# A new head for a grouped-query attention block with layer norms: host-laid-out weights, high parts stacked first, float32r masks, unrolled batches

## The reference, cut to what matters

```python
def layernorm(x, eps=1e-5): return (x - mean(x)) / sqrt(var(x) + eps)
def attn(x, wq, wk_down, wv_down, wk_up, wv_up, wo):      # x: (4, 1024, 256)
    q = x @ wq                                            # 8 heads of 128, 4 for each of 2 kv heads
    k = (x @ wk_down per kv head, 32 wide) @ wk_up        # to 128
    v = (x @ wv_down per kv head, 32 wide) @ wv_up
    p = softmax(where(causal, q @ k.T / sqrt(128), min))
    return (p @ v) @ wo
x = x + attn(layernorm(x), ...)
x = x + ffn(layernorm(x))
# the ffn is a routed attention whose softmax runs over the batch, followed by a layer norm with ln_g, ln_b
```

## Time and profile before

| | |
|---|---|
| runs, us | 547.71, 540.63, 546.01; median 546.01 |
| the profiled execution | 546.95 us, of which the span of the trace is 545.2 us |
| mean granted TensorE clock | 0.886 |
| PE busy | 479.8 us (88%) |
| DVE, ACT, POOL busy | 336.9, 227.2, 231.1 us |
| DMA | 27.29 MB, 50 GB/s over the span |

### The profile page before, as it was taken

How to read it: one execution, slowest core, us unless ns; L and a number is a source line. 1 busy time by engine, 2 the same in 40 slices (tenths; PEclk the granted TensorE clock), 3 DMA queues, 4 the chain that set the end, 5 groups by cost and what they waited for, 6 DMA issues and landing times.

```text
span 545.2 us, 8184 instructions
## 1 busy us (share of the span) xinstructions
PE 479.8 (88%) x2722; PEld 257.9 (47%) x2722; DVE 336.9 (62%) x513; ACT 227.2 (42%) x428; POOL 231.1 (42%) x166
## 2 busy tenths in 40 slices
PE   4869697989999979999999799999997998799671
PEld 3537354544465535544655455444654464334240
DVE  5443567475455897885456978875469689701423
ACT  2300221535445434554454445554554345456300
POOL 2110104024543564526433953375328445743922
PEclk9675757779999979999999899999999899989866
DMA  9790720003501441009005410073054100100011
GB/s 290 217 139 22 94 24 1 2 1 65 82 2 26 54 71 40 2 28 151 9 2 73 73 40 1 0 143 41 1 73 68 46 2 1 39 2 0 1 38 39
DMA packets 20910, 27.29 MB, mean 50 GB/s; under 512 B 2897, under 2 KB 12945, under 8 KB 20881
## 3 DMA queue, kind: packets, MB, share of 16 engines
q1 hardware_dynamic: 19584, 25.60, 25.7%
q10 hardware_dynamic: 1296, 1.31, 0.8%
HBM read 6.72 MB, written 4.19 MB: 20 GB/s over the span
## 4 chain that ended last, share of the span: by engine, by line
PE 59%; issue 15%; DVE 13%; DMA 4%; ACT 3%; POOL 3%; SPq 1%; ACTq 1%; POOLq 0%; DVEq 0%
PE st_ps L447 12%; PE mx_ps L465 12%; PE u_ps L487 10%; PE sh_ps L498 6%; DVE mx_part L814 5%; PE sh_ps L564 5%; PE mx_ps L469 3%; PE sh_ps L532 3%; DMA qs<-q_lo 3%; DVE y L894 2%; PE sh_ps L525 2%; DVE y L903 2%; PE sh_ps L537 2%; ACT pr L680 1%; DMA pr<-in_wq 1%
## 5 line engine op out<-in xcount | busy, mean ns | idle before, releaser
L814 DVE TENSOR_REDUCE mx_part<-mx_ps 128x2 f32<-128x1024 f32 (+3 forms) x160 | 176.5, 1114 | 95.2 <-PE mx_ps L469 66.1
L680 ACT ACTIVATE pr<-st_ps 128x512 f32<-128x512 f32 (+1 forms) x304 | 168.5, 574 | 154.5 <-PE st_ps L447 146.8
L1064 POOL TENSOR_TENSOR pr<-pr 128x768 f32<-128x768 f32 (+3 forms) x72 | 154.4, 2149 | 73.5 <-ACT pr L680 71.7
L465 PE MATMUL mx_ps<-ks,qs 96*128 96x512 f32 (+3 forms) x384 | 133.3, 426 | 23.3 <-DVE mx_part L814 16.9
L447 PE MATMUL st_ps<-qs,ks 98*128 98x512 f32 (+1 forms) x304 | 143.0, 485 | 5.1 <-ACT pr L680 3.5
L1051 POOL TENSOR_SCALAR_AFFINE_SELECT pr<-pr 128x512 f32<-128x512 f32 x64 | 43.3, 676 | 163.4 <-ACT pr L680 163.2
L465 PEld LDWEIGHTS mx_ps<-ks,qs 96*128 96x128 f32 x384 | 84.1, 224 | 40.3 <-DVE mx_part L814 28.1
L447 PEld LDWEIGHTS st_ps<-qs,ks 98*128 98x128 f32 x304 | 60.0, 203 | 85.0 <-ACT pr L680 42.4
L487 PE MATMUL u_ps<-pr,v 128*32 128x512 f32 (+3 forms) x768 | 88.5, 535 | 6.2 <-POOL pr L1051 6.2
L469 PE MATMUL mx_ps<-maskb,identb 128*128 128x128 bf16 x256 | 63.7, 255 | 0.0
L1042 POOL TENSOR_TENSOR rstd<-var,minus_half 128x4 f32<-128x4 f32 (+1 forms) x13 | 15.5, 1189 | 70.8 <-DVE var L845 55.2
(11 more groups left out here) (82 smaller groups left out, 361.7 us busy)
## 6 DMA issues: line engine op xcount, KB each, us to landing
qs<-q_hi SPq DMA_DIRECT2D x32, 256.0 KB, 5.6
qs<-q_lo SPq DMA_DIRECT2D x16, 256.0 KB, 6.9
out_y<-y SPq DMA_DIRECT2D x8, 512.0 KB, 3.0
x<-in_x SPq DMA_DIRECT2D x3, 1024.0 KB, 11.4
ks<-k_hi SPq DMA_DIRECT2D x32, 64.0 KB, 3.3
x<-in_x SPq DMA_DIRECT2D x2, 512.0 KB, 7.3
pr<-in_wq ACTq DMA_DIRECT2D x1, 1024.0 KB, 6.5
pr<-in_wo SPq DMA_DIRECT2D x1, 1024.0 KB, 8.8
```

The lines of the kernel that those rows point to most:

```text
L465: last = nc.tensor.matmul(bank[:, i * pitch:i * pitch + width], qs[g][0:KS, t // CT, h0 + i, t % CT * P:(t % CT + 1) * P], ks[g][0:KS, k0: ...
L680: nc.scalar.activation(pr[:, slot, h0:h0 + nh, off:CH], st_ps[n % 2][:, 0:nh * width].rearrange("p (h q) -> p h q", h=nh), ACT.Exp, scale= ...
L814: nc.vector.tensor_reduce(mx_part[:, t // CT, own, h0:h0 + nh, t % CT], mx_ps[n % 2][:, 0:nh * pitch].rearrange("p (h k) -> p h k", h=nh)[ ...
L1064: last = nc.gpsimd.tensor_tensor(even, even, pr[:, 6 + (e // 2) % 2, h0:h1, off:CH], ALU.add)
```

## The change

The host hands over `wq` by head and transposed, and the two up-projections transposed; the kernel loads them so, and the head's transposes of `wq` and `up` go. ACT starts the weight loads, SP those of x of batch 0, now in four pieces of two tiles. The head's order is new: x first, `wq` folded in two halves (`wq0`, `wq1`), `qb0` ahead of the first mx units, and four more mx units (6 to 9, `MX_EARLY`) in the head instead of the first window's first three tiles. x of batches 1 to 3 is loaded later, between and behind the stacks, and so are ln_g and ln_b. DMAs of high parts start when ACT has written the high part (`stack_hi`), those of low parts when DVE has written the low part (`stack_lo`), in the head and in every batch. The statistics of batch 1 stay at the head's end, those of batches 2 and 3 move to tile 1 of the second window of batches 0 and 1. The tiny `var` operations move from DVE to POOL, ahead of each power. The mask matmul takes float32r operands and covers all heads of a unit that lie in one PSUM bank (4, 2, 1, 1 heads at 128, 256, 384, 512 columns), 22 of them a window instead of 32. The loops are written out.

```diff
-MX_AT_FIRST = [5, 5, 4, 3, 2, 3, 3, 3, 2, 2, 1, 1]
+MX_AT_FIRST = [4, 4, 2, 3, 2, 3, 3, 3, 2, 2, 1, 1]
+MX_EARLY = 4
...
-USES_START = ["wqT0", "wqT1", "wqT2", "wqT3", "upT", "wq", "xT0", "xT1", "k0", "qa0", "xT2", "xT3",
-              "k1", "qa1", "wo", "v", "m0", "qb0", "qb1"]
-SETUP = USES_START.index("xT0")
+USES_START = ["xT0", "xT1", "k0", "wq0", "qa0", "xT2", "xT3", "k1", "qa1", "wq1", "qb0", "v", "m0", "qb1", "wo"]
...
+        minus_half = sb("minus_half", [P, TT])
         lng = sb("lng", [P, D])
         lnb = sb("lnb", [P, D])
         wqk = sb("wqk", [P, ND, NH * DL])
...
-            for c in range(NC):
-                sp.dma_start(x[:, 0, c * CT:(c + 1) * CT, :],
...
+            for i in range(2 * NC):
+                sp.dma_start(x[:, 0, 2 * i:2 * i + 2, :],
+                             x_d[0].rearrange("(i t p) d -> i p t d", t=2, p=P)[i]).then_inc(x0_in[i], 16)
             sp.dma_start(wo_in, wo_d.rearrange("(h p) n -> p h n", p=P)).then_inc(wo_loaded, 16)
-            for b in range(1, B):
...
+                for kind, g, c in pieces:
+                    s = slice(c * CH, (c + 1) * CH)
+                    if kind == "k":
+                        sp.wait_ge(hi_ready, nb * 6 + (1, 3)[c])
+                        for piece in (0, 2):
+                            sp.dma_start(ks[g][piece * DL:(piece + 1) * DL, s].bitcast(F),
+                                         k_hi[g * DL:(g + 1) * DL, s].bitcast(F)).then_inc(kstack_in[g][c], 16)
+                    else:
+                        sp.wait_ge(hi_ready, nb * 6 + ((2, 4), (5, 6))[g][c])
+                        for piece in (0, 1):
+                            sp.dma_start(qs[g][piece * DL:(piece + 1) * DL, c, :, :].bitcast(F), q_hi[:, s].bitcast(F)
+                                         ).then_inc(qstack_in[g][c], 16)
...
+            stack_hi(0, ("k", 0, 0), ("q", 0, 0))
+            wait_start(sp, "k0")
+            stack_lo(("k", 0, 0))
+            wait_start(sp, "qa0")
+            stack_lo(("q", 0, 0))
+            stack_hi(0, ("k", 0, 1), ("q", 0, 1))
+            wait_start(sp, "k1")
+            stack_lo(("k", 0, 1))
+            wait_start(sp, "qa1")
+            stack_lo(("q", 0, 1))
+            load_x(1)
+            stack_hi(0, ("k", 1, 0), ("q", 1, 0))
+            wait_start(sp, "qb0")
+            stack_lo(("k", 1, 0), ("q", 1, 0))
+            stack_hi(0, ("k", 1, 1), ("q", 1, 1))
+            wait_start(sp, "qb1")
+            stack_lo(("k", 1, 1), ("q", 1, 1))
             sp.dma_start(lng[:, :], lng_d[None, :].to_broadcast([P, D])).then_inc(ln_in, 16)
             sp.dma_start(lnb[:, :], lnb_d[None, :].to_broadcast([P, D])).then_inc(ln_in, 16)
...
-                s = slice(c * CH, (c + 1) * CH)
-                for piece, src in enumerate((q_hi, q_hi, q_lo)):
-                    sp.dma_start(qs[g][piece * DL:(piece + 1) * DL, c, :, :].bitcast(F), src[:, s].bitcast(F)
...
-            wait_start(sp, "k0")
-            stack_k(0, 0)
-            wait_start(sp, "qa0")
-            stack_q(0, 0)
-            wait_start(sp, "k1")
-            stack_k(0, 1)
-            wait_start(sp, "qa1")
-            stack_q(0, 1)
-            stack_k(1, 0)
-            stack_k(1, 1)
-            wait_start(sp, "qb0")
-            stack_q(1, 0)
-            wait_start(sp, "qb1")
-            stack_q(1, 1)
+            for b in range(2, B):
+                load_x(b)
...
-                stack_k(0, 1)
-                wait_apart(sp, (sh_read, use_no(b, 0, kind, "qa1") + 1))
-                stack_q(0, 1)
-                wait_apart(sp, (st_full, w * NST + (NST + ST_END[3])),
-                           (sh_read, use_no(b, 1, kind, "qb0") + 1))
...
+                sp.wait_ge(st_full, w * NST + ST_END[7])
+                stack_hi(b + 1, ("k", 0, 0), ("q", 0, 0))
+                sp.wait_ge(sh_read, use_no(b, 0, kind, "k0") + 1)
+                stack_lo(("k", 0, 0))
+                sp.wait_ge(sh_read, use_no(b, 0, kind, "qa0") + 1)
+                stack_lo(("q", 0, 0))
+                sp.wait_ge(st_full, w * NST + NST)
+                stack_hi(b + 1, ("k", 0, 1), ("q", 0, 1))
...
+                sp.wait_ge(st_full, w * NST + (NST + ST_END[7]))
+                stack_hi(b + 1, ("q", 1, 0), ("k", 1, 0))
+                sp.wait_ge(sh_read, use_no(b, 1, kind, "qb0") + 1)
...
-                    last = nc.tensor.matmul(bank[:, i * pitch:i * pitch + width],
-                                            qs[g][0:KS, t // CT, h0 + i, t % CT * P:(t % CT + 1) * P],
-                                            ks[g][0:KS, k0:k0 + width], start=True, stop=not own)
+                together = max(1, CH // pitch) if own else 1
+                for i0 in range(0, nh, together):
+                    heads = range(i0, i0 + together)
+                    for i in heads:
+                        last = nc.tensor.matmul(bank[:, i * pitch:i * pitch + width],
+                                                qs[g][0:KS, t // CT, h0 + i, t % CT * P:(t % CT + 1) * P],
+                                                ks[g][0:KS, k0:k0 + width], start=i == i0, stop=not own)
                     if own:
-                        last = nc.tensor.matmul(bank[:, i * pitch + width - P:i * pitch + width],
-                                                identb[:, :], maskb[:, :], start=False, stop=True)
+                        diagonals = bank[:, i0 * pitch:(i0 + together) * pitch].rearrange(
+                            "p (h k) -> p h k", h=together)[:, :, width - P:width]
+                        last = nc.tensor.matmul(diagonals, ident_r[:, :], mask_r[:, 0:together, :], start=False, stop=True)
                 last.then_inc(mx_full, 1)
...
             pe.sem_inc(pv_done, PV_AHEAD)
+            def fold(name):
+                starting(name)
+                if name == "wq0":
+                    pe.wait_ge(wq_in, 16)
+                g = int(name[-1])
+                for d in range(ND):
+                    for h in range(HG):
+                        last = nc.tensor.matmul(start_bank(name)[:, (d * HG + h) * DL:(d * HG + h + 1) * DL],
+                                                wqT[:, g * HG + h, d * P:(d + 1) * P], upT[:, 0, :], start=True, stop=True)
...
-            last.then_inc(sh_full, 1)
-            for name in USES_START[SETUP:]:
-                if name == "wo":
+            for name in USES_START:
+                if name == "v":
                     for i in range(MX_C0):
                         mx(0, 0, 0, i)
+                if name == "wo":
+                    for i in range(MX_C0, MX_C0 + MX_EARLY):
+                        mx(0, 0, 0, i)
+                if name[:2] == "wq":
+                    fold(name)
+                elif name == "wo":
...
-            wait_start(pe, USES_START[-2])
-            wait_start(pe, USES_START[-1])
+                else:
+                    fill(name, None, 0, 0, 0)
...
                         st(wn, 1 - g, n)
             batch(0, FIRST)
...
-            act.dma_start(wq_in_sb, wq_d.rearrange("(c p) n -> p c n", p=P)).then_inc(wq_in, 16)
+            act.dma_start(wkd[:, :, :], wkd_d.rearrange("(c p) n -> p c n", p=P)).then_inc(weights_in, 16)
+            act.dma_start(wvd[:, :, :], wvd_d.rearrange("(c p) n -> p c n", p=P)).then_inc(weights_in, 16)
+            act.dma_start(upT[:, :, :], up_d).then_inc(weights_in, 16)
...
                     last = nc.vector.bn_stats(st1[:, b, t, :], x[:, b, t, :])
-                last.then_inc(ln_step, 1)
-                dve.wait_ge(ln_step, 2 * count - 1)
+                last.then_inc(stats_step, 1)
+                dve.wait_ge(stats_step, count)
                 for t in tiles:
                     last = nc.vector.bn_aggr(mv1[:, b, t, :], st1[:, b, t, :])
-                last.then_inc(ln_step, 1)
-                dve.wait_ge(ln_step, 2 * count)
-                nc.vector.tensor_scalar(var1[:, b, tiles[0]:tiles[-1] + 1], mv1[:, b, tiles[0]:tiles[-1] + 1, 1], EPS, None,
-                                        ALU.add).then_inc(var_ready, 1)
+                last.then_inc(stats_ready, 1)
...
                     last = nc.vector.bn_aggr(mv2[:, t, :], st2[:, t, :])
-                last.then_inc(ln_step, 1)
-                dve.wait_ge(ln_step, steps + 2)
-                nc.vector.tensor_scalar(var2[:, :], mv2[:, :, 1], 1.0 + EPS, EPS * EPS, ALU.mult, ALU.add
-                                        ).then_inc(var_ready, 1)
+                last.then_inc(var_ready, 1)
             def norm2_apply(b, c, powers, steps, t, last_half):
...
                         dve.wait_ge(out_done, y_count(b, c) * 16)
...
+            nc.vector.memset(ones[:, :], 1.0).then_inc(consts_ready, 1)
             for c in range(NC):
-                dve.wait_ge(x0_in[c], 16)
-                norm1_stats(0, range(c * CT, (c + 1) * CT), c + 1)
-            for c in range(NC):
-                dve.wait_ge(rstd_ready, c + 1)
+                for i in range(2):
```

(34 more changed lines are left out.)

185 lines of the change are left out of this document (87 added, 98 removed).

## The result

The changed kernel takes **526.55 us** (median of 4 runs, 523.31 to 528.19) and the kernel before 546.12 (4 runs beside it, 540.63 to 547.71). The ratio is 0.9655, 95% interval [0.9596, 0.9713]: faster. The forecast was 531, with a range of 517 to 541.

What follows compares the result with a forecast made beforehand. PE, busy 88% of the span, was taken to set the pace, with its losses in the first 120 us. 546.95 - 4.9 (head) - 4.5 (units) - 2.0 (masks) - 4.6 (windows) + 0.3 (tail) = 531.3, so 531 us, range 517 to 541.

Steps and rivals of the forecast that it cites:

- The head: Start to resumption of DVE's maxima: earlier q_hi and SP's DMA queue move the resumption from 65.0 to 60.1, -4.9 us.
- my 60.1: Head: ln_b, last in SP's queue, lands at 24.0 + 2.65 + 33.4 = 60.1 us, when DVE resumes its maxima.
- v at half clock: Head: sign of being wrong; in the rival where the head gains nothing, resumption at 65, sum 536, chance 0.20.
- Four units less: First window of batch 0: mx units 6 to 9 leave its first three tiles, which ran at 0.50 clock, -4.5 us.
- Masks: Row-sum windows: grouped mask matmuls save 0.24 us a window, -2.0 us with the stretches at half clock.
- The "slower" rival: Masked matmuls: the float32r mask's weight load is never hidden, 176 x 0.137 = 24 us at full clock, total 559; chance 0.05.
- Windows: First windows of batches 1 to 3: var on POOL and earlier stacks save 1.3, 1.3 and 2 us, -4.6 us.
- The moved statistics: Second windows: 3.4 us of DVE and under 2 of POOL each cost 0; 5.4 each if nothing covered them.
- the gap of PE: Second windows: sign of being wrong, if the moved statistics open a gap of PE there.
- Loops: Windows: writing the loops out gains 0, since windows written out and inside the loop were 0.05 us apart.
- The clock, as a rival: First window: PE kept from falling to 1.2 GHz, up to 19 us gained, two thirds give 518; chance 0.15.

Runs made afterwards that it cites:

- experiment 6: Changed kernel with identity and mask in bf16 instead of float32r, masks still grouped: 526.22 us (521.91 to 529.37).
- experiment 4: Changed kernel without the four early mx units in the head, which go back into the first window: 529.04 us, one run of 536.78 left out.
- experiment 2: Changed kernel with the masks as before, bf16 and one matmul for each head: 526.09 us (523.27 to 528.45).
- experiment 3: Changed kernel with the variance's small operation back on VectorE: 529.31 us (528.77 to 533.97), one run of 538.54 left out.
- experiment 8: Changed kernel with each stack's three pieces copied together behind the low part: 524.25 and 516.72 us, runs of 526.63 and 531.70 left out.
- experiment 5: Changed kernel with x of batch 0 loaded in two pieces of 512 KB, not four of 256 KB: 518.41 us (516.41 to 521.49).
- experiment 7: Changed kernel without the moved statistics; batches 2 and 3 are normalised with those of batch 1: 517.64 us (512.35 to 518.36).
- experiment 10: Changed kernel with x in two pieces and idle matmuls at three kinds of places where TensorE waits: 517.48 us (515.26 to 517.77).
- experiment 9: Changed kernel, x in four pieces, with two idle memsets on VectorE delaying the first statistics by 0.9 us: 528.01 us (523.71 to 530.10).
- experiment 11: Changed kernel with x in two pieces and the layer norm's loads right behind wo_in: 520.77 us (517.96 to 524.97), one run of 527.34 left out.
- experiment 1: Changed kernel with the layer norm's gain and bias loads moved right behind wo_in: 526.18, 527.93, 528.08 us and one run of 515.28.

## Why the prediction was right, and where it was not

**The head (-4.9; it was -9.5).** The mechanism stands: the queue of copies decides, DVE waits for ln_b. From q's first copy to the resumption I had 36.1 us, and it was 34.7 (20.75 to 55.48). The step that failed is the start: I took the landing of x at 7.6 from the earlier trace rows and changed only the number of tiles behind it. x landed at 4.0, because the change also moves the small weights to ACT's queue ahead of wq (2.6 us, weights and wq together) and cuts the piece (0.9). Of these 3.6 us only 2.0 reached k, which began at 11.32 for my 13.3: the power covers four tiles and waits for the statistics of both pieces (rstd is used at 7.72, 3.7 us behind the first statistic, for my 2.4). And from k to q's high part it was 8.8 us for my 10.0, since PE had reached full clock by then (the four matmuls of q take 1.96 us, where they took 3.18 in the kernel before). That is 2.0 + 1.2 + 1.4 = 4.6 us under my 60.1, and the last two terms are partly luck: in the same head in experiment 6 k to q's high part took 9.5 us, and with v at half clock the maxima resumed at 58.70, nearer to my figure. I had named v at half clock as a sign of being wrong and priced it at a resumption of 65; it came in nine of the experiments' profiles, and since the whole head is earlier it costs about 3 us there and not the whole gain.

**Four units less (-4.5; the first window gave -7.4).** Taken alone they gave 2.5 us in the medians and 6.7 in the profiles (experiment 4), and my figure lies between. Over the window the clock is 0.80 in place of 0.76, which has its share in the 7.4; how large it is, no run shows.

**Masks (-2.0).** 0.24 a window by my sum, 0.3 by experiments 2 and 6 at full clock. In the total it can't be seen. The "slower" rival (weight load never hidden, 0.05) is refuted: the load is twice as long, and the window shows nothing of it.

**Windows (-4.6, from var and the stack together).** The variance is worth 1.3 us a window at full clock and 2.8 us in the medians, which is not clear of their spread (experiment 3); the stacks' order is worth nothing in the windows (experiment 8). So the 1.3 a window was of the right size and belongs to var alone. It shows where the clock is the same: the first window of batch 1 went from 55.74 us at 1.00 to 54.36 at 0.99, and the forecast said 54.5. The other two did not shrink. That of batch 2 takes 56.78 us at 0.97, where the kernel before had 55.73 at 1.00, and that of batch 3 takes 53.65 at 0.84, where it had 49.80 at 0.98. The step that failed is that I left the clock behind the first window as it was.

**The moved statistics (0).** Wrong: about 2 us, and the gap of PE that I had named as a sign of being wrong is there (4.52 us of idling, 3.57 without them). I argued from DVE's 37.43 busy us of 56.93; but in the second windows PE waits for DVE's maxima at places, and a share of busy time doesn't tell where.

**Loops (0).** The unrolled kernel was not run apart from the rest; the windows of both kernels agree only as far as the clock lets one see.

**The clock, as a rival (518, 0.15).** In the changed kernel it did not come true: 0.80 in the first window. Experiments 5, 7 and 10 reached its 518, but not by its way: in experiment 5 the first window's clock is 0.83, and the gain lies in the later windows, of which the rival did not speak. I had read their clocks of 0.94 and 1.00 as properties of the kernel. They are an outcome that small things turn over: experiments 5, 9 and 11 move loads or add 0.9 us of delay, and span 518 to 528 us.

What stays open is what decides the course. Experiment 5 has the better one in all four runs (516.41 to 521.49), and the same delay without its two pieces does not. But two pieces do not secure it (experiment 11, up to 527.34), and four do not bar it (experiment 7, 512.35 to 518.36, and single runs of experiments 1 and 8). In the profiles one thing goes with it. The first q's four matmuls take 1.96 us in the changed kernel and 2.7 to 3.4 in the eight whose profiled run took 525.87 us or more, but 3.75 in experiments 5 and 7, the two profiled runs with the better course and no fillers:

```profile
20.10 3.75 PE L531 MATMUL sh_ps<-xnT,wqk 128*128 128x512 f32 x4 [0.80 <-ACT wqk L748]
```

So there PE came to full clock latest. Two profiles are no proof, and I have no run that sets this moment by itself.

## What to carry to other kernels

Where PE is busy 88% and its clock moves between two levels, compare stretches at equal clock, not totals: here an edit that moved one landing by 0.9 us moved the total by 8 us, more than any term of the sum. A short wait of PE can cost itself and then what it does to the clock; harmless matmuls in the wait can be cheaper than the wait, even if they overrun it, and at the start of the program they brought the first real work to full speed. A timeline of one execution is one draw: set it beside those of other kernels with the same code there before you split a gain by it. And ask which other loads run beside the one that you time: their new order gave three times what cutting the load gave.

## What was unexpected of the hardware

- The granted clock reads 1.00 from the start of a program, but the first k (11.32) takes 3.65 us and the second (21.85) 1.90 for the same four instructions. With 6 us of fillers ahead, the first takes 1.90 as well. And in the kernel before, the first k (18.97) takes the same 3.65 us where the record does say half clock (the windows of k, before and after):

```profile
18.97:22.62 3.65, 3.65 (x5) 0.80 (x5) 0.43 (x5) 0.00 (x0) 1.64 (x1) 0.50 0.79 248
11.32:14.97 3.65, 3.65 (x5) 0.80 (x5) 1.43 (x5) 0.00 (x0) 1.27 (x2) 1.00 0.15 46
```

  So the first k of the changed kernel ran at half clock too. The record of the clock isn't to be trusted there; the durations are.
- Idle matmuls of 4.05 us in a wait of 2.60 us made the windows shorter, by 1.3 to 1.5 us against the changed kernel and by 1.8 and 1.9 against experiment 5 (54.32 for 56.07 us, 55.35 for 57.21).
- A VectorE operation on 128x4 elements lasted 4.03 us in three of eight places (0.17 in the others), and each time it ended with GpSimd's addition of 128x2048 elements (4.57 us); moved to GpSimd it takes 0.19.
- The float32r weight load of the mask takes 211 ns and the bf16 one 104, and the windows with either last the same (54.11 and 54.08 us).
